# A window of half a microsecond in a rehearsed order of five engines

## The chip, the cores and the metric

The kernel runs on one core of a Trainium2 chip. The metric is the device time of one execution in microseconds, taken as the median of several runs.

## The reference

A residual stream x of shape (8, 512, 256), so 8 batches of 512 tokens, goes through six blocks. Names in brackets are those of the kernel.

```
x = x + 0.5 * ffn0(layernorm(x))    # f0, round 1: 704 hidden, FP4 quantise/dequantise, silu(gate) * up
x = x + attn0(layernorm(x))         # a0: sigmoid q and k, decaying causal mixing over blocks of 128
x = x + 0.5 * ffn0(layernorm(x))    # f0, round 2
x = x + 0.5 * ffn1(layernorm(x))               # f1, round 1: soft mixture of 8 x 128 slots
x = x + attn1(layernorm(x))                    # a1: 16 heads of 16, causal softmax, LoRA on q, k, v, o
x = x + 0.5 * ffn1(layernorm(x))               # f1, round 2
```

(Each block gets the normalised x.) The parts that matter below:

```
# ffn1
logits = einsum(xn, slots)                       # 512 x 1024 for each batch
slots_in = einsum(xn, softmax(logits, over tokens))
h = gelu(slots_in @ w1);  processed = h @ w2     # hidden 1024
out = einsum(processed, softmax(logits, over slots))
# attn1
scores = q @ k.T / 4 + causal mask;  attn = softmax(scores);  out = lora(attn @ v, wo)
```

## The kernel before

Every stage of every block is written as a generator of **pieces**: a piece is what stands between two `yield`s, some waits followed by some instructions. An engine's program is a list of such generators (parts), for instance `a1_front`, `a1_first`, `a1_maxima`, `a1_second`, `a1_values` and `a1_out` on TensorE (PE), with counterparts on ScalarE (ACT), VectorE (DVE), GpSimd (POOL) and on SyncE (SP), which issues all DMAs. Within a part the order is fixed. Between the parts of one engine nothing is fixed: when the kernel is built, `rehearse` decides it.

`rehearse` plays the five programs against one another in a model (class `Rehearsal`: a duration for each operation; `LAG`: how long after an instruction its semaphore is seen, 200 ns for PE and 2200 ns for a DMA, whose issue costs 60 ns of SP). In `rehearsal`, each step looks at all pieces whose signals are known to come, on all engines; `start` tells when a piece could begin (its engine free, its semaphores come, its PSUM bank given back, 1283 ns more where ACT's table must change). The piece with the smallest pair (start, due time) is placed next. In the first of ten rounds the due time is the one written at the `yield`; in each later round it is what `latest` found, the latest finish that would not have moved the end of the round before. The order of the round with the shortest modelled end is kept, and `perform` writes each engine's instructions out in it. On the chip each engine runs its instructions in that order and stops at each wait that isn't yet met, with all that stands behind it. No time of the model remains, only the order.

The round 1 blocks f0 and a0 run first, batch by batch; then f0 round 2 mixed with f1 round 1; then a1 mixed with f1 of both rounds, and last f1 round 2 alone.

Two chains of a1 are used below. The matmul helper `three` (lines 714 to 716) makes each product from three f16 matmuls; transposes are on line 720.

- **The Q move.** `a1_front` projects q and k of a batch in two halves of the heads (c = 0, 1): `psum<-a1xT,a1wqh`. ACT and DVE write them to the staging tile a1st, and SP (`a1_moves`, line 689) spreads them into a1Q and a1K with six DMAs each. The move for half c of a batch may start only when the second-pass scores of the batch before have read that half (semaphore a1_s2), and the projection of the other half waits for the move (semaphores a1_q0, a1_q1), since it reuses the staging tile.
- **The maxima's move.** `a1_first` (line 990, with the masks on line 970) computes scores for DVE's row maxima; DVE puts them in a1mt, PE transposes them (`a1_maxima`), ACT copies them to a1mr (line 1404), and SP writes them with four DMAs (line 697) into a row of a1Q (semaphores a1_m0, a1_m1). `a1_second` (line 1020) computes the scores again, now less their maximum, for ACT's exponential (a1PT, line 1415). Its first group of a half waits for that move. Line 1043 is probabilities times values, lines 1139 to 1141 are f1's sums over tokens, and line 1122 spreads f1's column maxima.

Of the kernel before, what the change touches and what calls it, by code (L numbers as in the profile page):

```python
# [263 lines left out]


LAG = {"pe": 200.0, "act": 130.0, "dve": 110.0, "pool": 100.0, "sp": 2200.0}
ROUNDS = 10


# [19 lines left out]
def rehearse(programs, sems):  # L289

    late, best = None, None
    for _ in range(ROUNDS):
        order, end, late = rehearsal(programs, sems, late)
        if late is None:
            break
        if best is None or end < best[1]:
            best = order, end
    return best


def latest(done, end):

    users, last = {}, {}
    for i, (key, work, needs) in enumerate(done):
        if key[:2] in last:
            users.setdefault(last[key[:2]], []).append((i, 0.0))
        last[key[:2]] = i
        for j, offset in needs:
            if j != i:
                users.setdefault(j, []).append((i, offset))  # L310
    sources, left, room = {}, [len(users.get(i, ())) for i in range(len(done))], [0.0] * len(done)
    for j, those in users.items():
        for i, offset in those:
            sources.setdefault(i, []).append((j, offset))
    clock = {key[0]: 0.0 for key, _, _ in done}
    ready = {en: [] for en in clock}
    for i, n in enumerate(left):
        if not n:
            ready[done[i][0][0]].append(i)
    out = {}  # L320
    while len(out) < len(done):
        t, _, en, i = min((max(clock[en], room[i]), -i, en, i) for en in ready for i in ready[en])
        ready[en].remove(i)
        clock[en] = t + done[i][1]
        out[done[i][0]] = end - clock[en]
        for j, offset in sources.get(i, ()):
            room[j] = max(room[j], clock[en] - offset)
            left[j] -= 1
            if not left[j]:
                ready[done[j][0][0]].append(j)  # L330
    return out


def rehearsal(programs, sems, late):

    names = {id(v): k for k, v in sems.items()}
    parts, order, clock, table = {}, {}, {}, None
    for en, program in programs.items():
        notes = []
        q = Queue(None, sems, notes)  # L340
        parts[en] = [Part(i, g, notes) for i, g in enumerate(program(Rehearsal(en, names, notes), q, Banks(q)))]
        order[en], clock[en] = [], 0.0
    came, maker, done = {k: [] for k in sems}, {k: [] for k in sems}, []
    port = {"dve": 0.0, "pool": 0.0}

    def due(en, part):
        return part.due if late is None else late.get((en, part.at, part.n), part.due)

    active = {}
    held, freed = set(), {}  # L350
    blocked, ready = {}, {en: [] for en in programs}

    def missing(part):
        own = {}
        for n in part.piece:
            if n[0] == "wait" and n[1] != "dve" and len(came[n[1]]) + own.get(n[1], 0) < n[2]:
                return n[1]
            if n[0] == "op" and n[3]:
                own[n[3]] = own.get(n[3], 0) + n[4]
        return None  # L360

    def file(en, part):
        if part.due is None:
            return
        name = missing(part)
        if name is None:
            ready[en].append(part)
        else:
            blocked.setdefault(name, []).append((en, part))

    def start(en, part):
        t = clock[en]
        for n in part.piece:
            if n[0] == "wait" and n[1] != "dve":
                if len(came[n[1]]) >= n[2]:
                    t = max(t, came[n[1]][n[2] - 1])
            elif n[0] == "take":
                if n[1] in held:
                    return None
                if n[1] in freed:  # L380
                    name, value = freed[n[1]]
                    if len(came[name]) < value:
                        return None
                    t = max(t, came[name][value - 1])
            elif n[0] == "op":
                if n[2] is not None and n[2] != table:
                    t += 1283
                return t
        return t

    for en in programs:
        for part in parts[en]:
            file(en, part)
    while True:
        best = None
        for en in programs:
            for part in ready[en]:
                t = start(en, part)
                if t is not None and (best is None or (t, due(en, part)) < best[0]):
                    best = ((t, due(en, part)), en, part)  # L400
        if best is None:
            break
        (t, _), en, part = best
        began, needs, me, work = t, [], len(done), 0.0
        signals = []
        for n in part.piece:
            if n[0] == "wait":
                if n[1] == "dve":
                    t += 30
                else:  # L410
                    t = max(t, came[n[1]][n[2] - 1])
                    needs.append((maker[n[1]][n[2] - 1], work - 130.0))
            elif n[0] == "take":
                held.add(n[1])
                if n[1] in freed:
                    name, value = freed[n[1]]
                    needs.append((maker[name][value - 1], -200.0))
            elif n[0] == "after":
                held.discard(n[1])
                freed[n[1]] = (n[2], n[3])  # L420
            else:
                if n[2] is not None:
                    table = n[2]
                slow = en == "pe" and active.get(int(t // 3413.3) - 1, 0) < 3060
                if n[5]:
                    active[int(t // 3413.3)] = active.get(int(t // 3413.3), 0) + n[5]
                if n[6]:
                    t = max(t, port["pool" if en == "dve" else "dve"])
                t += 2 * n[1] if slow else n[1]
                work += n[1]  # L430
                if n[6]:
                    port[en] = t
                if n[3]:
                    came[n[3]] += [t + LAG[en]] * n[4]
                    maker[n[3]] += [me] * n[4]
                    signals.append(n[3])
        done.append(((en, part.at, part.n), work, needs))
        clock[en] = t
        order[en].append(part.at)
        ready[en].remove(part)  # L440
        part.step()
        file(en, part)
        for name in signals:
            again = blocked.pop(name, [])
            for en2, part2 in again:
                file(en2, part2)
    left = sorted((p.due, en, p.gen.__name__, p.piece[:3]) for en in programs for p in parts[en] if p.due is not None)
    assert not left or late is not None, (left[:25], held, [v for v in freed.items()])
    if left:
        return order, 0.0, None  # L450
    end = max(clock.values())
    return order, end, latest(done, end)
# [1708 lines left out]
```

## Time and profile before

| | us |
|---|---|
| median of 3 runs | 2682.31 |
| lowest, highest | 2676.18, 2683.8 |
| the profiled execution, its own time | 2685.53 |
| its span in the profile | 2683.7 |
| PE busy | 2355.7 (88%) |
| DVE busy | 1890.2 (70%) |
| ACT busy | 1594.0 (59%) |
| POOL busy | 880.0 (33%) |
| PE's mean granted clock | 0.959 of full speed |

Shares of busy time are means over the whole span. A busy PE counts the time in which a matmul is in the array, so the real spacing of matmuls is read from their starts. The views used below are the page's busy times, a table of stretches of the span, the list of who waited for whom, and the instructions in order of time.

### The profile page before, as it was taken

The numbers are of one execution on the slowest core, as the hardware profiler recorded it, in microseconds if no ns is written. First come the engines' busy times: TensorE is split into PE (matmuls) and PEld (weight loads), VectorE is DVE, ScalarE is ACT, GpSimd is POOL, SyncE is SP. The second block draws the span as 40 slices with busy tenths as digits, with TensorE's granted clock in tenths as the row PEclk, the third lists the DMA queues.
The fourth block names the chain that finished last, engine by engine and source line by source line (L and its number), as shares of the span: only waits on it lengthen the run. The fifth ranks groups of instructions, "written<-read, shape, count | busy, mean of one in ns | idle before, by whom it ended". The sixth has DMA issues, their size and how long they took to land.

```text
span 2683.7 us, 54388 instructions
## 1 busy us (share of the span) xinstructions
PE 2355.7 (88%) x22748; PEld 1802.2 (67%) x22748; DVE 1890.2 (70%) x3345; ACT 1594.0 (59%) x2643; POOL 880.0 (33%) x631
## 2 busy tenths in 40 slices
PE   1788898987999988989898999899897989998997
PEld 1456666666777776667676777576666677776786
DVE  6689999998797967777676767778676665444331
ACT  2244654657667474775656486666576466666653
POOL 0112212212323321362535364544436155122222
PEclk9789999999999999999998999999998999998999
DMA  4000000000000000000000000000000000000000
GB/s 162 26 1 1 1 1 1 1 1 1 1 1 1 1 1 25 4 23 2 13 14 13 14 14 14 13 14 2 33 2 25 10 4 7 9 9 1 9 9 9
DMA packets 34836, 33.07 MB, mean 12 GB/s; under 512 B 7648, under 2 KB 33952, under 8 KB 34592
## 3 DMA queue, kind: packets, MB, share of 16 engines
q1 hardware_dynamic: 34592, 29.60, 3.4%
q8 instruction: 180, 2.95, 0.5%
q14 instruction: 64, 0.52, 0.1%
HBM read 12.54 MB, written 4.19 MB: 6 GB/s over the span
## 4 chain that ended last, share of the span: by engine, by line
PE 65%; DVE 20%; ACT 7%; issue 4%; POOL 2%; SPq 1%; DMA 1%; POOLq 0%; DVEq 0%; ACTq 0%
PE psum L714 17%; PE psum L715 15%; PE psum L716 15%; PE psum L720 5%; PE psum L1139 2%; PE psum L990 2%; PE psum L1141 2%; PE psum L1140 2%; PE psum L1043 2%; PE psum L1020 1%; POOL a1pr L2102 1%; ACT a1PT L1415 1%; DVE f0hT L1722 1%; DVE f1e L1979 1%; DVE a1pr L1864 1%
## 5 line engine op out<-in xcount | busy, mean ns | idle before, releaser
L2115 POOL TENSOR_TENSOR f1hT<-f1g,f1hT 128x512 f16<-128x512 f32 x256 | 308.2, 1209 | 707.1 <-ACT f1hT L1518 706.8
L2102 POOL TENSOR_TENSOR a1pr<-a1PT,a1pr 128x1024 f16<-128x1024 f32 (+1 forms) x176 | 358.2, 2038 | 309.6 <-DVE a1pr L1864 309.6
L714 PE MATMUL psum<-f1sl,f1w1h 128*128 128x256 f16 x1024 | 287.6, 281 | 32.4 <-ACT f1g L1513 18.9
L714 PE MATMUL psum<-f1w2h,f1hT 128*128 128x256 f16 x1024 | 280.5, 274 | 7.1 <-POOL f1hT L2115 5.5
L715 PE MATMUL psum<-f1sl,f1w1h 128*128 128x256 f16 x1024 | 286.6, 280 | 0.0
L716 PE MATMUL psum<-f1sl,f1w1l 128*128 128x256 f16 x1024 | 286.4, 280 | 0.0
L715 PE MATMUL psum<-f1w2l,f1hT 128*128 128x256 f16 x1024 | 279.6, 273 | 0.0
L716 PE MATMUL psum<-f1w2h,f1hT 128*128 128x256 f16 x1024 | 279.6, 273 | 0.0
L1841 DVE TENSOR_REDUCE a1nm<-psum 128x2 f32<-128x768 f32 (+3 forms) x176 | 198.3, 1126 | 76.4 <-PE psum L970 75.3
L2091 POOL TENSOR_TENSOR f0h<-f0Y,f0sc 128x704 f32<-128x704 f32 x64 | 93.2, 1456 | 415.5 <-DVE f0Y L1710 415.5
L1864 DVE CAST a1pr<-a1PT 128x1024 f16<-128x1024 f32 (+1 forms) x176 | 161.8, 924 | 72.0 <-ACT a1PT L1415 56.3
L1513 ACT ACTIVATE f1g<-psum 128x512 f32<-128x512 f32 x256 | 152.4, 595 | 90.2 <-PE psum L716 80.8
L1415 ACT ACTIVATE a1PT<-psum 128x1024 f32<-128x1024 f32 (+1 forms) x176 | 166.5, 946 | 56.3 <-PE psum L970 34.9
L714 PE MATMUL psum<-wguh,f0xT 128*128 128x352 f16 x512 | 166.0, 324 | 34.9 <-DVE f0xT L1676 21.3
L715 PE MATMUL psum<-wgul,f0xT 128*128 128x352 f16 x512 | 165.4, 323 | 0.0
L716 PE MATMUL psum<-wguh,f0xT 128*128 128x352 f16 x512 | 165.1, 322 | 0.0
L1518 ACT ACTIVATE f1hT<-f1g 128x512 f16<-128x512 f32 x256 | 161.5, 631 | 5.5
L1139 PE MATMUL psum<-f1xnh,f1e 128*128 128x257 f16 x512 | 142.4, 278 | 13.6 <-DVE f1d L1975 9.7
L714 PE MATMUL psum<-f1pr,f1eT 128*128 128x256 f16 x512 | 140.0, 273 | 2.9 <-DVE f1pr L2022 2.6
L714 PEld LDWEIGHTS psum<-f1sl,f1w1h 128*128 128x128 f16 x1024 | 102.9, 100 | 58.3 <-ACT f1g L1513 23.8
L1141 PE MATMUL psum<-f1xnh,f1e 128*128 128x257 f16 x512 | 141.3, 276 | 0.0
L1140 PE MATMUL psum<-f1xnl,f1e 128*128 128x256 f16 x512 | 140.4, 274 | 0.0
(315 smaller groups left out, 6864.1 us busy)
## 6 DMA issues: line engine op xcount, KB each, us to landing
a1Q<-a1st SPq DMA_DIRECT2D x96, 64.0 KB, 2.6
a1K<-a1st SPq DMA_DIRECT2D x96, 64.0 KB, 2.6
x<-in_L_attn_x SPq DMA_DIRECT2D x8, 512.0 KB, 7.7
out<-x SPq DMA_DIRECT2D x8, 512.0 KB, 3.0
wslot<-in_L_ffn_w SPq DMA_DIRECT2D x1, 1024.0 KB, 8.7
wraw<-in_L_ffn_w SPq DMA_DIRECT2D x1, 1024.0 KB, 5.7
wslot<-in_L_ffn_slot_embeds SPq DMA_DIRECT2D x1, 1024.0 KB, 8.0
a1Q<-a1mr SPq DMA_DIRECT2D x64, 4.0 KB, 1.7
```

Of the source, the lines that this page charges most:

```text
L714: e.matmul(out, lh, rh, start=start, stop=False)
L715: e.matmul(out, lh, rl, start=False, stop=False)
L716: return e.matmul(out, ll, rh, start=False, stop=stop)
L1139: e.matmul(v[:, 0:D + 1], e1[:, jp % 2, 0, t, es], xn_h[:, t, 0:D + 1], start=t == 0, stop=False)
L1140: e.matmul(v[:, 0:D], e1[:, jp % 2, 0, t, es], xn_l[:, t, :], start=False, stop=False)
L1141: ins = e.matmul(v[:, 0:D + 1], e1[:, jp % 2, 1, t, es], xn_h[:, t, 0:D + 1], start=False, stop=t == NT - 1)
L1415: e.activation(a1["PT"][:, i % 2, :, 0:w], psum[:, 0:2, 0:w], ACT.Exp).then_inc(s["a1_ex"])
L1518: e.activation(hT1[:, 0, 2 * hp:2 * hp + 2, :], g2, ACT.Copy).then_inc(s["f1_hh"])
L1841: e.tensor_reduce(out, src, AX, ALU.max, negate=True).then_inc(s["a1_m"])
L1864: e.tensor_copy(a1["pr"][:, i % 2, 0, :, 0:w], a1["PT"][:, i % 2, :, 0:w]).then_inc(s["a1_ph"])
L2102: e.tensor_tensor(a1["pr"][:, i % 2, 1, :, 0:w], a1["PT"][:, i % 2, :, 0:w], a1["pr"][:, i % 2, 0, :, 0:w], ALU.subtract).then_inc(s["a1_pl"])
L2115: e.tensor_tensor(hT1[:, 1, 2 * hp:2 * hp + 2, :], gg[:, hp % 2, :, :], hT1[:, 0, 2 * hp:2 * hp + 2, :], ALU.subtract).then_inc(s["f1_hl"])
```

## The change

A new constant and a new rule for the choice of the next piece. For each engine, all pieces that can begin within 500 ns of the earliest one are looked at, and the one with the least due time among them is the engine's candidate, even if it begins later. Between engines the candidate with the smallest (start, due time) goes next, as before.

```diff
 LAG = {"pe": 200.0, "act": 130.0, "dve": 110.0, "pool": 100.0, "sp": 2200.0}
+WINDOW = 500.0
 ROUNDS = 10
...
         best = None
         for en in programs:
-            for part in ready[en]:
-                t = start(en, part)
-                if t is not None and (best is None or (t, due(en, part)) < best[0]):
+            can = [(t, part) for t, part in ((start(en, part), part) for part in ready[en]) if t is not None]
+            if can:
+                first = min(t for t, _ in can) + WINDOW
+                t, part = min(((t, part) for t, part in can if t <= first), key=lambda z: (due(en, z[1]), z[0]))
+                if best is None or (t, due(en, part)) < best[0]:
                     best = ((t, due(en, part)), en, part)
         if best is None:
             break
```

No instruction of the stages is added or taken away, apart from ACT's table loads (152 before, 148 after), which depend on the order. Line numbers below line 264 grow by 3. Nearly every stretch of every engine's order differs; two places are shown.

**PE, the end of batch 5's second pass for head half 0, and batch 6's projection of q for half 1.** Before: the last second-pass group of half 0 (first three rows), and the projection that waits for the Q move.

```order
L1020 MATMUL psum<-a1Q,a1K 128x128 [waits s_a1_ex]
L1020 MATMUL psum<-a1Q,a1K 128x128 x7
L970 MATMUL psum<-cst 128x64 x4
L1043 MATMUL psum<-a1V,a1pr 128x33 [waits s_a1_pl]
L1043 MATMUL psum<-a1V,a1pr 128x33 x15
L1122 MATMUL psum<-f1mr,idb 128x128 [waits s_f1_ss]
L1122 MATMUL psum<-f1mr,idb 128x128 x3
L1020 MATMUL psum<-a1Q,a1K 128x128 [waits s_a1_ex,s_a1_m1]
...
L714 MATMUL psum<-a1xT,a1wqh 128x512 [waits s_a1_cl,s_a1_q0]
```

After, the same group and the same projection:

```order
L1023 MATMUL psum<-a1Q,a1K 128x128 [waits s_a1_ex]
L1023 MATMUL psum<-a1Q,a1K 128x128 x7
L973 MATMUL psum<-cst 128x64 x4
L717 MATMUL psum<-f1sl,f1w1h 128x256 [waits s_f1_pl]
...
L717 MATMUL psum<-f1sl,f1w1h 128x256
L718 MATMUL psum<-f1sl,f1w1h 128x256
L719 MATMUL psum<-f1sl,f1w1l 128x256
L717 MATMUL psum<-a1xT,a1wqh 128x512 [waits s_a1_cl,s_a1_q0]
```

Between the group and the projection stood 44 short matmuls; now 84 matmuls of 256 to 512 columns of f1 stand there beside 56 short ones.

**PE, the last batch: the turn of the maxima of half 0, and the first second-pass group.** Before (the group, which waits for s_a1_m0, stands some 200 rows further on):

```order
L720 MATMUL psum<-cst,a1mt 64x128 [waits s_a1_xu,s_a1_mt]
L720 MATMUL psum<-cst,f1u 128x128 [waits s_f1_Tl,s_f1_ex]
L720 MATMUL psum<-cst,f1u 128x128 x3
L990 MATMUL psum<-a1K,a1Q 128x384 [waits s_a1_m]
L990 MATMUL psum<-a1K,a1Q 128x384
L970 MATMUL psum<-cst 128x64 x4
L714 MATMUL psum<-f1sl,f1w1h 128x256 [waits s_f1_pl]
...
L1020 MATMUL psum<-a1Q,a1K 128x128 [waits s_a1_m,s_a1_m0]
```

After:

```order
L723 MATMUL psum<-cst,a1mt 64x128 [waits s_a1_xu,s_a1_mt]
L1142 MATMUL psum<-f1xnh,f1e 128x257 [waits s_f1_ds,s_f1_el,s_f1_nl]
L1143 MATMUL psum<-f1xnl,f1e 128x256
L1144 MATMUL psum<-f1xnh,f1e 128x257
...
L1023 MATMUL psum<-a1Q,a1K 128x128 [waits s_a1_m,s_a1_m0]
L1023 MATMUL psum<-a1Q,a1K 128x128
L973 MATMUL psum<-cst 128x64 x4
```

Twelve matmuls of about 256 columns now stand between the turn and the group that needs its result, where 20 transposes, 168 long matmuls and 36 matmuls of score groups stood.

## Rows read from the trace of the kernel before

**Rows 1.** The page: busy us, share of the span and instructions of each engine.

```profile
PE 2355.7 (88%) x22748; PEld 1802.2 (67%) x22748; DVE 1890.2 (70%) x3345; ACT 1594.0 (59%) x2643; POOL 880.0 (33%) x631
```

**Rows 2.** Stretches of the span: length, busy us (instructions) of each engine, PE's clock, DMA.

```profile
core 0: us, PE busy (x) PEld busy (x) DVE busy (x) ACT busy (x) POOL busy (x), PEclk, DMA share, GB/s
0.00:134.00 134.00, 56.87 (x252) 37.22 (x252) 85.12 (x153) 36.22 (x57) 12.53 (x16) 0.90 0.30 94
134.00:603.00 469.00, 415.09 (x2929) 291.94 (x2930) 433.54 (x854) 248.56 (x424) 100.14 (x91) 0.96 0.00 1
603.00:1073.00 470.00, 430.52 (x3502) 340.18 (x3500) 378.12 (x660) 298.67 (x478) 132.32 (x107) 0.98 0.01 5
1073.00:2214.00 1141.00, 1033.23 (x12503) 792.90 (x12500) 811.88 (x1372) 732.21 (x1222) 517.74 (x323) 0.96 0.04 13
2214.00:2684.00 470.00, 419.97 (x3576) 339.99 (x3570) 181.52 (x311) 278.31 (x464) 117.31 (x95) 0.94 0.02 8
```

**Rows 3.** PE's waits over the span: us in total, times, longest us.

```profile
PE psum L1020 <- ACT a1PT L1415: 32.8, 39, 4.7
PE psum L714 <- DMA a1Q<-a1st: 23.5, 7, 4.6
...
PE psum L990 <- DMA a1K<-a1st: 2.3, 1, 2.3
```

**Rows 4.** PE in order of time: start us, length us, instruction.

```profile
1877.12 0.27 PE L1140 MATMUL psum<-f1xnl,f1e 128*128 128x256 f16 x1
1877.23 0.27 PE L1141 MATMUL psum<-f1xnh,f1e 128*128 128x257 f16 x1
```

**Rows 5.** PE in order of time, idle us before a row in brackets.

```profile
1880.53 0.22 PE L970 MATMUL psum<-cst 64*128 64x64 bf16 x4
...
1887.18 0.61 PE L714 MATMUL psum<-a1xT,a1wqh 128*128 128x512 f16 x1 [4.57 <-DMA a1Q<-a1st]
```

**Rows 6.** SP's queue in order of time, the same place.

```profile
1880.84 4.28 SPq L689 DMA_DIRECT2D a1Q<-a1st  x6
```

**Rows 7.** The page's DMA issues: count, KB each, median us to landing.

```profile
a1Q<-a1st SPq DMA_DIRECT2D x96, 64.0 KB, 2.6
...
a1Q<-a1mr SPq DMA_DIRECT2D x64, 4.0 KB, 1.7
```

**Rows 8.** Stretches behind three of the Q waits, columns as in rows 2.

```profile
1887.00:1890.00 3.00, 2.81 (x8) 1.08 (x9) 0.00 (x0) 0.04 (x1) 1.57 (x1) 0.50 0.32 109
1286.00:1293.00 7.00, 6.28 (x51) 4.32 (x52) 2.37 (x4) 3.44 (x5) 0.25 (x1) 0.52 0.16 54
1463.00:1474.00 11.00, 9.34 (x139) 6.87 (x137) 7.65 (x17) 7.31 (x12) 6.05 (x4) 0.53 0.06 20
```

**Rows 9.** In order of time: the turn of the maxima, the copy, the four issues.

```profile
2114.94 0.30 PE L720 MATMUL psum<-cst,a1mt 128*64 128x128 f32 x1
...
2115.74 0.26 ACT L1404 ACTIVATE a1mr<-psum 64x128 f16<-64x128 f32 x1
2116.03 2.44 SPq L697 DMA_DIRECT2D a1Q<-a1mr  x4
```

**Rows 10.** Groups of instructions: count, busy us, mean ns of one, idle before.

```profile
L1513 ACT ACTIVATE f1g<-psum 128x512 f32<-128x512 f32 x256 | 152.4, 595 | 90.2 <-PE psum L716 80.8 <-POOL f1hT L2115 6.0
L1518 ACT ACTIVATE f1hT<-f1g 128x512 f16<-128x512 f32 x256 | 161.5, 631 | 5.5
L2115 POOL TENSOR_TENSOR f1hT<-f1g,f1hT 128x512 f16<-128x512 f32 x256 | 308.2, 1209 | 707.1 <-ACT f1hT L1518 706.8
L1415 ACT ACTIVATE a1PT<-psum 128x1024 f32<-128x1024 f32 (+1 forms) x176 | 166.5, 946 | 56.3 <-PE psum L970 34.9 <-POOL a1pr L2102 20.5
L1500 ACT ACTIVATE f1eT<-psum 128x512 f16<-128x512 f32 x128 | 76.3, 596 | 64.6 <-PE psum L720 64.1
L2004 DVE TENSOR_TENSOR f1eT<-psum,f1eT 128x512 f16<-128x512 f32 x128 | 87.5, 684 | 48.8 <-ACT f1eT L1500 48.7
```

**Rows 11.** ACT in order of time, around one table load.

```profile
1209.20 0.27 ACT L1431 ACTIVATE a1cT<-psum 128x128 f16<-128x128 f32 x1
1209.49 1.28 ACT L1465 ACT_TABLE_LOAD   x1
1210.78 1.06 ACT L1465 ACTIVATE f1d<-f1d 128x1024 f32<-128x1024 f32 x1
```

## The prediction

> **What bounds the kernel now.** I read the page's busy shares first, then a table of stages, then the waits of PE. The page gives PE 88% of the span, DVE 70%, ACT 59% [rows 1], but these are averages over four stages [rows 2]. Up to 134 us the weights arrive and are prepared: PE is busy 56.9 of 134 us. From 134 to 603 us the f0 and a0 blocks run: DVE is busy 433.5 of 469 us (92%) and sets the pace; PE's gaps there are cover for DVE. From 603 us on PE is the bound (430.5 of 470, 1033.2 of 1141, 420.0 of 470 us), with DVE at 80, 71 and 39%. Total work is the same in the changed kernel, so only idle time and PE's clock can move. PE's idle time from 603 us on is 39.5 + 107.8 + 50.0 = 197.3 us, and its granted clock there is 0.98, 0.96 and 0.94.
>
> The waits of PE in that stretch [rows 3] fall into two sorts. Many small ones wait for ACT, DVE or POOL: 32.8 us in 39 waits for the exponential, to name the largest. A few large ones wait for a DMA: 23.5 us in 7 waits for the move of Q rows, and 2.3 us once for K.
>
> Matmuls of 256 columns start 0.11 us apart [rows 4]. So the order itself tells how much PE work lies between two of its rows: I call that cover. A wait shows where the cover is shorter than the latency that it has to hide. I take latencies from the trace, cover from the order of before and after, and compare the two.
>
> **Part 1: the Q move, a gain.** SP may move the new Q rows only after the last second-pass score group of the earlier head half. In batch 6 (the eight are counted from 0) that group's masks end at 1880.75 [rows 5], SP issues six DMAs from 1880.84 on, which takes 4.28 us [rows 6], the landing adds 2.6 us [rows 7], and PE starts the projection that waits for it at 1887.18: 6.4 us, of which 4.57 were idle. The rehearsal prices such a move at 6 x 0.06 + 2.2 = 2.6 us, so it believes 1 to 3 us of cover to be enough. Before has covers of 4.0, 3.5, 2.2, 5.5, 1.8, 1.1 and 2.2 us at batches 1 to 7. After has 7.1, 16.6, 4.4, 22.0, 7.0, 11.7 and 16.1: the most urgent work (the second pass) is ahead of the projections, which stand later. Against 6.4 us one batch is short, by 2.0. At batch 0 the order changes too: K's cover is 3.9 us, against one activation, one DVE row, six issues and a landing, so some 4 us of stall, where the K wait of [rows 3] now stands with one of the seven Q waits ahead of it. DMA stalls fall from 23.5 + 2.3 = 25.8 to 2.0 + 4 = 6 us: **-20 us**.
>
> After such a stall PE's granted clock is at the lower of its two levels, 1.2 GHz: 0.50 over 1887 to 1890, 0.52 over 1286 to 1293, 0.53 over 1463 to 1474 [rows 8]. That is 1.5 + 3.4 + 5.2 = 10.1 us of full-rate time lost behind three of the seven. The longer spans hold other stalls as well, and new stalls (part 2) bring some back; I take **-8 us**.
>
> **Part 2: the maxima's move, a loss.** The first second-pass group of a batch waits for the turned row maxima: PE transpose, ACT copy, four DMAs of 4 KB. At the last batch the transpose starts at 2114.94 and takes 0.30, the copy ends at 2116.00 and the four issues take 2.44 us from 2116.03 [rows 9]; the last begins 0.6 us before that is over and lands 1.7 us later [rows 7], at 2119.6. That is 4.4 us after the transpose. Before hides this everywhere: its covers are 7.9, 16.4, 18.5, 17.8, 9.0, 21.0, 21.6 and 27.2 us. After, the second pass is the urgent work, and the rehearsal prices the move at 2.4 us and the whole path near 3: the covers are 4.8, 4.5, 2.1, 4.3, 2.5, 7.1, 3.4 and 1.3 us. Shortfalls against 4.4: 2.3 + 0.1 + 1.9 + 1.0 + 3.1 = 8.4 us. Behind the waiting matmul stands all of PE's queue, since an engine runs its rows in order. ACT's copy may also stand behind another piece of 0.6 us or a table load of 1.28 us [rows 11] at one batch or another, which I put at 3 us in all: **+11 us**.
>
> **Part 3: tighter loops, both signs.** An urgent piece is now waited for up to half a microsecond, so PE gets to the consumer with less work done in between. GELU, copy and subtraction take 0.60 + 0.63 + 1.21 = 2.4 us [rows 10]; covers too short for that (under 2.5) rise from 6 to 16 of 256. The exponential takes 0.95 [rows 10]; covers below 0.99 rise from 33 to 46 of 176. The f1 transposes of the second softmax need 0.60 + 0.68 = 1.3 [rows 10]; short ones rise from 16 to 28 of 128. A loop's latency in the trace runs from PE's signal to the signal that PE waits for. Adding the shortfalls of all loops behind the last a0 block in PE's order, at the shortest tenth of each loop's latencies, gives 56 us before and 77 after: **+21 us**. Only 56 of the 171 us of PE's idle time that is not DMA is explained this way; the rest is queueing, a result that waits on ACT or DVE behind less urgent work. The same window shortens that: ACT work between GELU and its copy falls from 0.82 to 0.71 us in the mean, PE work from the first to the second matmul group of the MLP from 8.3 to 7.7, from slots to their transposes from 4.4 to 3.2; between the two DVE steps of the dispatch weights it grows from 5.6 to 6.7. I take a tenth of 171: **-17 us**. The bounds are zero and the 115 us of queueing times a quarter, 29.
>
> **Part 4: the small terms.** In the stage that DVE bounds, the DVE work ahead of the last a0 update grows from 537 to 547 us, and that of f0's second round falls from 936 to 928: a swap of work that must be done anyway, cover for the one being the other. Taken at 0, with 10 us to either side. At the start, 5 us of attention weights leave the stretch of DVE ahead of the last quantised weight; but PE's first gate matmul has 54 us of DVE work ahead of it, where it had 52. Taken at 0, bounds -5 to +5. ACT's table loads fall from 152 to 148: 4 x 1.28 = 5.1 us [rows 11] of an engine that is busy 59%, so **-2 us**.
>
> The Trainium skill ("ScalarE: Activation LUTs", What ACT_TABLE_LOAD costs) adds a drain of 1.38 us to each load, 2.66 in all; here the load starts 0.02 us after the activation ahead of it has ended, and the one behind starts 0.01 us after the load [rows 11], so the rows speak against a drain. By the page the four loads would be 10.6 us of ACT and the term -4 in place of -2.
>
> **Sum.** -20 - 8 + 11 + 21 - 17 - 2 = -15 us. From the profiled execution's 2685.5 us (span 2683.7) that is 2670.5; that execution is 3.2 us above the median of 2682.3, so the forecast is 2667 us, 0.6% faster.
>
> **Rivals.**
> (a) No change: the saved DMA stalls come back. PE reaches the projection later, but what follows it (scores, softmax) was waited for elsewhere, and parts 2 and 3 eat the rest. For it: the work is the same, and the milestones of PE work keep their places within 1% (the end of the last a1 block at 1794 us of PE work before and 1788 after). It gives 2682, +-8.
> (b) Slower: the half microsecond is spent on the engine that is the bound. PE idles by plan for urgent pieces, and queues do not shrink, since what shortens one chain lengthens another (the dispatch weights above). Place: the score and softmax groups between 1073 and 2214 us, where PE waits for the exponential. At the median latencies of the trace in place of the shortest tenth, the shortfalls from 603 us on are 159 us before and 230 after: +71 us in place of +21 - 17. Then -20 - 8 + 11 + 71 - 2 = +52: 2734. With half of that increase it is 2699. It decides once covers lost weigh more than about 30 us net of the queues. The Trainium skill ("Perfetto Trace Analysis", Optimization Strategies) bears on this: the goal is to keep the matmul engine at high utilization. Waiting on purpose on PE goes against it; by that rule the time would be that of this rival, and the trace agrees with the rule so far as PE is busy over 90% from 603 us on.
> (c) Much faster: the queue term is larger, since waits also drop PE's clock. Tripled (-51) and with the clock at 0.98 throughout instead of 0.96 and 0.94 (0.02 x 1141 + 0.04 x 470 = 42 us, half of it taken), the sum is -70 and the time 2612.
> (d) The window does not do what it says: the rehearsal keeps the best of ten rounds by its own model, and its best round may owe nothing to urgency. The covers above differ in one direction at all eight batches, so it does act; I fold this into (a).
>
> **How the numbers follow.** Forecast 0.37, (a) 0.20, (b) 0.33, (c) 0.10. The range has to reach (b) in its milder half and nearly all of (c): 2620 to 2722; the forecast's own range, from its bounds, is 2640 to 2680. Faster by over 0.3% (about what a measurement of this kernel can tell from no change): 0.46; within 0.3%: 0.19; slower: 0.35.
>
> **What would show it.** Right: PE's waits for the Q move fall from 23.5 us to under 8; a new wait of PE for the maxima's rows, 6 to 15 us at several batches; PE busy time unchanged within 10 us. Part 3 is wrong if PE's waits for ACT, DVE and POOL together grow or shrink by over 20 us. Wrong as a whole if PE's idle time from 603 us on does not fall although the Q waits do: then (b). If DVE's idle time before 603 us changes by over 10 us, part 4 was mis-sized.

## The result and the profile after

The changed kernel takes 2636.7 us (median of 4 runs, 2634.7 to 2646.8), beside 2683.1 for the kernel before (median of 4 runs on the same chip): a ratio of 0.9837, interval 0.9803 to 0.987, or 44 us less (35 to 53). The forecast was 2667. Its sign held, and the size was a third of what came: -15 against -44. The whole range (2620 to 2722) held; the forecast's own (2640 to 2680) was missed by 3 us, and the result lies halfway between the forecast and rival (c). The profiled execution took 2637.7 us with a span of 2635.9. In what follows a time difference is always the ratio's, times 2681 to 2683.

The page of the changed kernel, which answers to [rows 1]:

```profile
PE 2349.1 (89%) x22748; PEld 1795.1 (68%) x22748; DVE 1912.8 (73%) x3345; ACT 1594.3 (60%) x2639; POOL 868.2 (33%) x631
```

The same 22748 matmuls are busy for 7 us less. The same stretches of time as [rows 2], columns as there; since the program is now shorter, the last stretch ends at 2635.9:

```profile
0.00:134.00 134.00, 62.18 (x311) 44.37 (x312) 88.76 (x164) 39.76 (x65) 15.24 (x18) 0.85 0.29 94
134.00:603.00 469.00, 408.18 (x2879) 287.60 (x2877) 434.73 (x845) 247.49 (x417) 99.75 (x89) 0.97 0.00 1
603.00:1073.00 470.00, 436.17 (x3510) 337.89 (x3511) 383.98 (x663) 298.81 (x476) 126.04 (x107) 0.96 0.01 5
1073.00:2214.00 1141.00, 1045.66 (x12633) 798.29 (x12632) 830.64 (x1376) 736.71 (x1234) 526.38 (x333) 0.97 0.04 13
2214.00:2684.00 470.00, 396.94 (x3421) 326.91 (x3419) 174.68 (x300) 271.58 (x448) 100.81 (x86) 1.00 0.02 7
```

Nothing is won where DVE is the bound: the last a0 update ends at 571.8 us, before at 567.7, and the first f1 block ends at 796.1, before at 797.0. The last a1 block ends 19.8 us earlier (2255.4 for 2275.2), and what follows is another 28 us shorter. So there are two gains: about 20 us in the a1 stage and the rest behind it.

PE's waits over the span, which answer to [rows 3]:

```profile
PE psum L1023 <- ACT a1PT L1418: 17.0, 27, 1.6
...
PE psum L1046 <- DVE a1c L1886: 10.2, 8, 2.4
...
PE psum L1023 <- DMA a1Q<-a1mr: 1.8, 2, 1.3
...
PE psum L717 <- DMA a1Q<-a1st: 0.3, 1, 0.3
```

The Q wait is gone (23.5 to 0.3 us) and that for the exponential is halved (32.8 to 17.0), while the wait for the context rows (a1c) has grown from 2.0 to 10.2. The wait for the turned maxima, which the prediction put at 11 us, is 1.8.

The stretch from the end of the last a1 block to the end of the program holds the last experts' layers alone. It is the best place to read, since it has some 3000 matmuls in either kernel. Before:

```profile
2275.20:2683.70 408.50, 363.31 (x2991) 296.48 (x2989) 148.31 (x249) 236.54 (x388) 86.19 (x75) 0.95 0.02 8
```

and after:

```profile
2255.40:2635.90 380.50, 356.15 (x3000) 291.11 (x2998) 155.00 (x270) 238.77 (x395) 85.01 (x74) 1.00 0.02 8
```

PE's idle time in it (length less busy) falls from 45.2 to 24.4 us, and its granted clock rises from 0.95 to 1.00, so that nearly the same matmuls (3000 and 2991) are busy for 7 us less.

### The profile page after: what moved, and what is told of

The parts are those of the page before. It is cut to its first block, busy times and chain, and to the rows that moved or that the text cites. A ratio compares the mean times of both kernels' runs of the same rounds, so it can differ in the third digit from the quotient of the medians.

```text
span 2635.9 us, 54364 instructions
## 1 busy us (share of the span) xinstructions
PE 2349.1 (89%) x22748; PEld 1795.1 (68%) x22748; DVE 1912.8 (73%) x3345; ACT 1594.3 (60%) x2639; POOL 868.2 (33%) x631
## 4 chain that ended last, share of the span: by engine, by line
PE 62%; DVE 22%; ACT 7%; issue 4%; POOL 3%; SPq 1%; DMA 1%; DVEq 0%; POOLq 0%; ACTq 0%
PE psum L717 16%; PE psum L719 15%; PE psum L718 15%; PE psum L723 5%; PE psum L1142 2%; DVE a1pr L1867 2%; PE psum L1144 2%; PE psum L1143 2%; PE psum L993 2%; PE psum L1046 2%; POOL a1pr L2105 2%; DVE a1nm L1844 1%; DVE f1d L1978 1%; PE psum L1023 1%; ACT a1PT L1418 1%
## 5 line engine op out<-in xcount | busy, mean ns | idle before, releaser
L2105 POOL TENSOR_TENSOR a1pr<-a1PT,a1pr 128x1024 f16<-128x1024 f32 (+1 forms) x176 | 350.3, 1991 | 428.4 <-DVE a1pr L1867 428.3
L1867 DVE CAST a1pr<-a1PT 128x1024 f16<-128x1024 f32 (+1 forms) x176 | 180.5, 1026 | 67.0 <-ACT a1PT L1418 46.5
L1503 ACT ACTIVATE f1eT<-psum 128x512 f16<-128x512 f32 x128 | 76.0, 594 | 120.1 <-PE psum L723 119.3
```

Source lines behind the costliest of these rows:

```text
L1867: e.tensor_copy(a1["pr"][:, i % 2, 0, :, 0:w], a1["PT"][:, i % 2, :, 0:w]).then_inc(s["a1_ph"])
L2105: e.tensor_tensor(a1["pr"][:, i % 2, 1, :, 0:w], a1["PT"][:, i % 2, :, 0:w], a1["pr"][:, i % 2, 0, :, 0:w], ALU.subtract).then_inc(s["a1_pl"])
```

## The experiments

Line numbers in the runs' rows are up to nine higher than in the kernel before. Where only a window or a price is changed, the rest of the scheduler is that of the changed kernel, and a window of 0 gives the order of before.

### The two gains, one at a time

The first pair uses the window in a last pass of the rehearsal, on one side only of the end of the last a1 block. The window behind it alone:

```diff
-WINDOW = 500.0
+WINDOW, LATER = 0.0, 500.0
+        used = late
...
-            best = order, end
-    return best
+            best = order, end, used
+    order, end, _ = rehearsal(programs, sems, best[2], True)
+    return order, end
...
-                first = min(t for t, _ in can) + WINDOW
+                first = min(t for t, _ in can) + (LATER if final and len(came["a1_xu"]) >= 4 * B else WINDOW)
```

> The order is that of the kernel before on every engine until the last a1 block is rehearsed (PE's first differing instruction is number 20325 of 23374); only behind it does the half-microsecond window act, so only the last experts' layers are in another order. Theory A (about half of the gain is made in the last stage, by the window itself): PE's gaps behind 2214 us fall from 45.5 to about 21 us and its clock loss from 27.5 to about 2, and the time is 2683 - 24 = about 2659. Rival B (the last stage gained only because the state handed over to it by the a1 stage was better, or by luck of the rounds): within 6 us of before, about 2680.

Measured: 0.9933 (0.9912 to 0.9954), -18 us, short of the 24 expected and far from nothing. The same stretch of this run, with the same 2991 matmuls as before:

```profile
2266.80:2655.50 388.70, 351.86 (x2991) 289.66 (x2988) 147.68 (x249) 244.83 (x395) 85.63 (x75) 0.99 0.02 8
```

408.5 us have become 388.7: 8.4 us of it is idle time (45.2 to 36.8), and 11.4 is PE's busy time at a clock of 0.99 in place of 0.95. Not all of the clock is the window's: this execution reached the stretch 8.4 us earlier than before did (2266.8 for 2275.2), in an order that is still the same up to there (see the last section). Which waits went is seen in PE's waits of that stretch, before:

```profile
PE psum L720 <- ACT f1u L1495: 11.7, 9, 2.0
PE psum L714 <- DVE f1pr L2022: 8.5, 8, 1.9
PE psum L1139 <- DVE f1d L1975: 5.5, 6, 2.2
PE psum L714 <- ACT f1g L1513: 4.1, 2, 2.6
```

and with the window behind the last a1 block:

```profile
PE psum L719 <- DVE f1pr L2027: 6.2, 8, 1.4
PE psum L725 <- ACT f1u L1500: 5.3, 4, 1.5
PE psum L725 <- DVE f1d L1951: 4.8, 2, 2.6
...
PE psum L1144 <- DVE f1d L1980: 1.7, 2, 0.9
```

What fell most is the wait for the exponentials that PE turns (f1u, 11.7 to 5.3 us), then those for f1g (4.1 to 1.1, below these rows) and f1pr (8.5 to 6.2); those for f1d, at three lines now, rose from 5.5 to 7.8. They are waits for results of ACT and DVE, where the window lets an urgent piece pass others.

The complement is the same edit with the two numbers exchanged (`WINDOW, LATER = 500.0, 0.0`):

> The complement: the order of the changed kernel until the last a1 block, and no window behind it (PE's first instruction that differs from the changed kernel is number 20544). Theory A (two separate gains that add): the a1 stage's 20 us stay and the last stage's are lost, 2683 - 22 = about 2661. Rival B (the last stage's gain comes with what is handed over to it): close to the changed kernel, 2637 to 2645. If both this and the tail alone stay near 2680, the gains need each other.

Measured: 0.9921 (0.9905 to 0.9937), -21 us. The two halves sum to -39, the whole change is -44 (35 to 53): they add, within what can be measured. By its times rival B falls on both sides: 2664 where it gave about 2680, 2662 where it gave 2637 to 2645. In the profile a part of it stays open. The last stretch of this run, where no window acts, is 398.5 us long, 10 less than before:

```profile
2257.10:2655.60 398.50, 358.55 (x3000) 293.69 (x2997) 155.88 (x270) 230.47 (x390) 85.43 (x74) 0.98 0.02 8
```

Of the 10 us 5 are idle time (45.2 to 40.0) and 5 are busy time at the higher clock. So of the 28 us by which the changed kernel is shorter here, the timed runs give the window in this stretch about 18.

### The Q stalls by themselves

The clean test of part 1 keeps every engine's order as it was before, and takes away only what the wait is for. The wait protects a buffer: the projection of the second head half goes into the `a1st` slot that the first half's move still reads. With a slot for each half it is not needed. The rehearsal still sees the old wait, so it writes the old order.

```diff
+        st2 = sb("a1st2", [P, 2, 2, T], f16)
...
-                    q.wait_ge(f"a1_{'qk'[k_]}{1 - c}", 96 * (b + c))
+                    if isinstance(e, Rehearsal):
+                        q.wait_ge(f"a1_{'qk'[k_]}{1 - c}", 96 * (b + c))
+                    else:
+                        q.wait_ge(f"a1_{'qk'[k_]}{c}", 96 * b)
...
-                    e.activation(a1["st"][:, i % 2, 0, :], psum[:, 2 + i % 2, :], ACT.Copy, scale=(0.25, 1.0)[k] / WS).then_inc(s["a1_sh"])
+                    e.activation((a1["st"], st2)[c][:, k, 0, :], psum[:, 2 + i % 2, :], ACT.Copy, scale=(0.25, 1.0)[k] / WS).then_inc(s["a1_sh"])
```

(and the same two edits where ACT waits, DVE subtracts and SP moves).

> The kernel before, every engine's order kept word for word, but with a second buffer for the projected Q and K rows, so that PE's projections no longer wait for the move of the rows before: the Q stall (23.5 us in 7 waits) is taken away and nothing else. Theory S (my prediction's: such a stall is worth its time and the slow clock behind it): 2681 - 20 to -28, so 2653 to 2661. Rival T (in the a1 stage a stall that goes lets PE run into the next wait, since ACT and DVE are nearly as far behind): PE's waits for the exponential, for POOL and DVE, or for the moved rows at the first pass, grow by 12 to 20 us, and the time is 2672 to 2681.

Measured: 0.9909 (0.9895 to 0.9924), -24 us (20 to 28). By its time theory S holds. PE's waits from 1073 to 2214 us in this run:

```profile
PE psum L1027 <- ACT a1PT L1424: 35.2, 42, 4.7
PE psum L997 <- DVE a1nm L1850: 9.8, 14, 2.7
PE psum L718 <- ACT f1g L1522: 7.3, 8, 3.2
PE psum L1050 <- POOL a1pr L2111: 6.7, 9, 1.3
```

In the kernel before the same four are 31.4, 9.4, 7.4 and 5.3 us, beside 20.8 for the Q move. Of 20.8 us only 5.5 came back at these four. The seventh stall, ahead of this stretch at batch 0, came back whole: where 2.7 us for Q and 2.3 for K stood, PE now stands for 5.5 us before its first score group. And the clock behind the stalls returned in part: the stretch from 1286 to 1293 us of [rows 8], at 0.52 there, is at 1.00 here, that from 1463 to 1474 is at 0.85 for 0.53, and 1870 to 1890 is at 1.00.

```profile
1286.00:1293.00 7.00, 5.21 (x56) 4.37 (x57) 5.80 (x12) 4.46 (x9) 5.20 (x4) 1.00 0.14 48
```

The profiled executions tell where the time went. From 603 us to the end of the last a1 block (2275.2 before, 2253.4 here) PE's idle time fell from 151.8 to 138.9 us and its busy time by 9 us, from 1520.4 to 1511.5. So about half of the stall time was won as idle time, and the higher clock added 9 us; theory S has the sum right, while rival T has a share in it. How much of the 9 us is owed to the stalls is open, since the clock differs by as much between executions of one order (see the last section). Another 6 us lie in the last stretch, in the same order, and are the clock's (see the last section).

### Is it luck of the order?

The rehearsal's lag of PE's signals is set to 201 ns in place of 200, without a window (`"pe": 201.0`, `WINDOW = 0.0`):

> No window; the rehearsal's lag of PE's signals is 201 ns in place of 200, which moves nothing on purpose and still gives another order (PE's from instruction 113 on). It shows how far two equally aimed orders lie apart. Its cover between the last score group and the projection that waits for the moved Q rows is as short as in before (0 to 4.9 us at the batches 1 to 7). Theory (the gain is the window's): the Q waits stay at 20 to 30 us and the time is 2683 +- 8. Rival (the 46 us are luck among orders): orders scatter by as much as the gain, so this one may lie anywhere between 2640 and 2720.

Measured: 1.002 (1.0006 to 1.0034), +5 us, with 22.1 us of Q waits in 8 times. Another order aimed in the same way gives nearly the same time. The same jitter with the window (`"pe": 201.0`, `WINDOW = 500.0`):

> The changed kernel (window 500 ns) with PE's lag at 201 ns in place of 200: the window's second order, as the jittered run was the second order without it. Its cover ahead of the Q projections happens to be 1.3 to 3.5 us, as short as in before, so the Q waits come back in full, 20 to 30 us. Theory W (the window's gain is shorter waits for ACT and DVE, in the a1 and the last stage): 2630 to 2655 all the same, with PE's waits for the exponential near 17 us and not 32. Theory S: 2637 + 23 = 2660. Rival L (luck of orders): 2665 to 2700.

Measured: 0.9916 (0.9895 to 0.9936), -22 us. The Q waits are back and the waits for the exponential stay short:

```profile
PE psum L717 <- DMA a1Q<-a1st: 20.8, 7, 4.5
...
PE psum L1023 <- ACT a1PT L1418: 14.2, 26, 1.8
```

The time alone does not split the theories: 2656 was measured, theory S gave 2660 and theory W at most 2655. PE's idle time by stages does. From 603 us to the end of the last a1 block it is 151.8 us before, 147.2 here (1655.9 less 1508.7) and 129.8 in the changed kernel (1652.4 less 1522.6); behind that block it is 45.2, 28.9 and 24.4. So theory W is right only in the last stage. The changed kernel is 21 us faster than this run, and its Q waits are 20.5 us less. So the waits for the exponential, 32.8 us before, 17.0 after and 14.2 here, bought nothing that others (a1c, 8.5 us here) did not take back, and the Q stalls are what the a1 stage had to give. **That the window removes them is not assured**: the first order under the window did it, the second did not. Half of the -44 us is thus owed to which order came out; two orders with the window lie 22 us apart, two without it 5.

### Which engine must choose?

Behind the last a1 block again, but the window acts on PE's choice alone, or on that of the other four alone. The edit adds `and en == "pe"` (or `en != "pe"`) to the condition of the first experiment.

> As the run with the window behind the last a1 block only, but there it acts on PE's own choice alone; ACT, DVE, POOL and SP take the earliest piece as before (the order of before until PE's instruction 20325). The tail alone with the window on all engines gave a ratio of 0.9933, -17.5 us. Theory Q (the gain is a shorter queue in front of ACT and DVE: the urgent one of two results that lie there is served first): PE's choice adds little, 0 to -5 us, 2677 to 2682. Rival P (PE's choice carries it: it hands the urgent chain's matmuls out first): -12 to -17 us, 2665 to 2670.

> The complement: behind the last a1 block the window acts on ACT, DVE, POOL and SP, and PE takes the earliest piece as before. Theory Q: -12 to -17 us, 2665 to 2670. Rival P: 0 to -5 us, 2677 to 2682. If both reach about -17, either engine's choice is enough, since each rehearsed order then fits itself to the other; if neither does, the two need each other.

Measured: PE alone 0.9976 (0.9965 to 0.9987), -6 us; the others alone 0.9987 (0.9975 to 1.0), -3 us; both together -18. Neither theory holds: each half gives about a third or less. The two seem to need each other, but the 8 us by which they fall short together are only little more than what these intervals can tell (about 7). The stretch behind the last a1 block, PE alone:

```profile
2274.40:2673.00 398.60, 357.16 (x2991) 291.93 (x2988) 147.65 (x249) 249.80 (x399) 85.84 (x75) 0.97 0.02 8
```

and the others alone:

```profile
2274.60:2678.30 403.70, 360.52 (x2992) 294.85 (x2989) 147.73 (x250) 242.40 (x392) 86.62 (x75) 0.96 0.02 8
```

Idle 41.4 and 43.2 us, beside 45.2 without and 36.8 with all. A chain of the softmax passes PE, ACT and DVE in turn, and what it gains at one engine it loses in the next one's queue. That reading fits the rows, but no run shows it link by link.

### The size of the window

`WINDOW = 250.0`:

> Half the window. Cover ahead of the Q projections 4.0, 5.8, 0.9, 2.6, 4.6, 6.4 and 3.9 us (shortfalls 16.7 us). Theory W (a dose: some urgency helps, a microsecond is far too much): between the two, 2645 to 2670. Rival L (orders scatter and the size means little below a microsecond): outside of that.

Measured: 0.9893 (0.9873 to 0.9913), -29 us, with 10.3 us of Q waits. `WINDOW = 1000.0`:

> The window doubled to a whole microsecond. Cover ahead of the Q projections is 20.8 to 28.9 us at all batches, so no Q waits; cover between the turning of the maxima and the first second-pass group is 11.9 us at batch 0 and 0.3 to 3.3 at the other seven, against a path of 4.2 to 4.8. Theory M (cover counted in PE work is a floor; PE's ordinary waits and slow clock lengthen it by 1 to 3 us a batch, as in the changed kernel): the waits for the maxima's rows grow from 2.5 to between 8 and 18 us, and the time is 2645 to 2660. Rival 1 (more urgency is more gain): 2625 to 2637. Rival 2 (PE idles by plan for up to a microsecond, in all loops): 2670 or more, with PE's waits for ACT, DVE and POOL up by over 20 us.

Measured: 1.0261 (1.0243 to 1.0278), **+70 us**. Rival 2 holds. No Q wait is left, and yet it is the slowest of all. PE's waits from 1073 to 2330 us, most of its a1 stage (the last a1 block ends at 2400.5):

```profile
PE psum L1046 <- POOL a1pr L2105: 26.8, 48, 1.0
PE psum L1023 <- ACT a1PT L1418: 25.0, 44, 1.5
PE psum L993 <- DMA a1K<-a1st: 9.9, 3, 3.8
```

and the stretch itself:

```profile
1073.00:2330.00 1257.00, 1113.66 (x12925) 838.38 (x12924) 869.10 (x1433) 778.98 (x1283) 532.14 (x339) 0.93 0.04 12
```

PE waits 48 times for POOL's probabilities, 0.6 us each, where the changed kernel does so 13 times in its a1 stage (8.1 us). I read them as waits by plan, an urgent piece being awaited for up to a microsecond while others could run; none is longer than 1.0 us. The clock is 0.93 where it was 0.97. The loss is not in this stretch alone: before 603 us PE is idle for 148 us (131 before) and has 171 fewer matmuls behind it. The last stage kept its gain: from 2330 us to the end PE is busy for 399.6 of 419.2 us, at a clock of 1.00. Summed over the span, PE's idle time is 355 us (287 in the changed kernel, 328 before), and the time lost to the lower clock, the span times one less its mean granted clock (0.945, 0.966, 0.959), is 151 us (90 and 110). My theory M named a wait of 8 to 18 us for the maxima; in PE and its weight loads it is 3.8 and 5.7 us, wrong.

So the results are 0, -29, -44 and +70 us for windows of 0, 250, 500 and 1000 ns, with one order for each but 0 and 500. The second order at 500 ns gave -22, so these runs do not tell whether 250 or 500 is better; the +70 lies far outside of that scatter.

### The price instead of the window, and both

The rehearsal prices a DMA's issue at 60 ns, and six took 4.28 us [rows 6]. With 600 ns and no window:

```diff
-        return self.note(60)
+        return self.note(600)
```

> No window; one number of the rehearsal's prices is changed instead: the issue of a DMA costs 600 ns, near the measured six issues in 4.28 us, in place of 60. The covers ahead of the Q projections become 6.4, 6.2, 7.0, 4.0, 2.9, 10.3 and 4.2 us, against 6.4 needed, where before has 4.0, 3.5, 2.2, 5.5, 1.8, 1.1 and 2.2. Theory (the Q stalls are worth their time, whoever takes them away): shortfalls fall from 24.6 to 8.3 us, PE's Q waits to about 8 us, the time to 2683 - 16 - 5 = 2662. Rival (saved Q stalls come back elsewhere): Q waits fall just so, and the time stays within 6 us of 2683.

Measured: 0.9922 (0.9901 to 0.9942), -21 us. The Q waits fall to 2.4 us, the time as theory S says. But the place does not: from 1073 to 2214 us PE's idle time is 106.4 us, for 107.8 before, at the same clock of 0.96. Up to 603 us it is 118.5 for 131.0, and from there to 1073 it is 30.5 for 39.5; behind 2214 us the clock is 0.97 for 0.94. The price moves every order, the start's too, so this run does not tell the theories apart; the one with the second buffer does.

> The changed kernel's window with the rehearsal's DMA issue at 600 ns in place of 60. Its order happens to have short covers again ahead of the Q projections: 4.0, 13.5, 2.4, 3.7, 2.6, 3.5 and 4.8 us against 6.4 needed, shortfalls 17.4 us where the changed kernel has 2.0. Theory S (the gain of the a1 stage is the Q stalls'): Q waits come back with 10 to 16 us, the last stage stays fast, and the time is 2637 + 15 = 2652. Rival T (the window's gain in the a1 stage is shorter queues): 2632 to 2642 although the Q waits return.

Measured: 0.9803 (0.9782 to 0.9823), -53 us, 2625.7 us: the fastest kernel of the study. Both theories were too slow. Its Q waits are back in part, short ones:

```profile
PE psum L717 <- DMA a1Q<-a1st: 8.5, 6, 2.8
```

and its last stretch of [rows 2] is as good as the changed kernel's: PE's idle gaps there are 19.7 us (20.7), its clock 1.00. The medians put it 11 us under the changed kernel, and the intervals of the two ratios overlap, so that it is the faster of the two isn't certain. Taking its Q waits away as well, with the second buffer and the same order:

> The order of the run with both the window and the DMA price (2625.7 us), with the second buffer, so without its Q waits of 8.5 us. Theory S: 2626 - 9 = 2615 to 2619. Rival T: 2622 to 2626.

Measured: 0.9812 (0.9792 to 0.9831), -50 us, no gain. The 8.5 us of waits are gone, and nothing is gained: PE's idle time from 1073 to 2214 us is 97.3 us with them and 99.3 without. The time, 2631, is above even rival T's 2622 to 2626. The two ratios can be told apart to within 8 us, so a gain of up to 5 us is not excluded, but theory S's 9 is. Six stalls of 1.4 us in the mean were slack here; seven of 3.4 in the mean (the kernel before) were not.

## Why the prediction was right in sign and too small

**Part 1, Q move (-20, and -8 for the clock): right.** The waits fell by 23.2 us, and the stalls with the clock behind them are worth -24 (20 to 28) in the order of before, for -28 forecast. PE's projections at batches 1 to 7 wait once, 0.3 us. The wait of about 4 us at batch 0 came: PE stands for 3.1 us before its first score group, at 1029.7 (the profile names no releaser for it).

**Part 2, maxima (+11): wrong, by about 9 us.** The path was sized rightly. From the start of PE's transpose to the last landing it takes 4.2 to 4.8 us at the eight batches; the prediction's 4.4 us, which count from the end of the transpose, are 4.7 from its start. What failed is "Shortfalls against 4.4": I compared the path with a cover counted in PE work. A cover is a floor of the time between two rows. To it comes every ordinary wait in between, and every stretch at the lower clock. From the transpose to the first second-pass group 7.3, 9.5, 5.5, 7.7, 4.8, 14.3, 5.2 and 4.4 us went by, of which 0.3 to 3.7 were other waits and up to 2.0 clock. Batch 7 in order of time, where the cover was shortest (1.3 us by the prediction):

```profile
2079.67 0.40 PE L723 MATMUL psum<-cst,a1mt 128*64 128x128 f32 x1 [0.31 <-DVE x L1894]
2080.10 0.27 ACT L1407 ACTIVATE a1mr<-psum 64x128 f16<-64x128 f32 x1
...
2080.39 9.37 SPq L700 DMA_DIRECT2D a1Q<-a1mr  x8
...
2084.03 0.10 PEld L1023 LDWEIGHTS psum<-a1Q,a1K 50*128 50x128 f16 x2 [0.99 <-DMA a1Q<-a1mr]
2084.03 0.23 PE L1023 MATMUL psum<-a1Q,a1K 50*128 50x128 f16 x2 [0.51 <-DMA a1Q<-a1mr]
```

PE's clock in between:

```profile
2081.00:2084.00 3.00, 2.53 (x12) 1.46 (x10) 1.22 (x3) 2.31 (x4) 0.00 (x0) 0.54 0.03 6
```

Twelve matmuls stand 0.21 us apart where [rows 4] have 0.11, so they cover twice the time. PE stood for 0.51 us, where 3.1 were forecast. Its only other wait for these rows is 1.3 us at batch 4, where 1.9 were forecast, and the 3 us booked for a late copy show in no wait for these rows.

**Part 3, tight loops (+21) and queues (-17): wrong, and where most of the missing gain lies.** In the head the two nearly cancel, as forecast: the head alone gives -21, the Q stalls -24. In the last stage they do not, and the window there gives -18. The term was one figure for all stages, "a tenth of 171". Counted in the orders as the prediction counts (an estimate of mine that no view of the profile shows), the shortfalls behind the last a1 block are 17 us before and 16 after, about equal. So what is left there as queueing is 45 - 17 = 28 us before and 24 - 16 = 8 after. By that estimate it fell by 70% in that stage. Elsewhere it hardly moved: from 603 us to the end of the last a1 block PE's idle time less its waits for DMAs is 126.0 us before (151.8 less 25.8) and 124.6 after (129.8 less 5.2, the 3.1 us at batch 0 counted with them). There PE is the bound, with DVE busy 36% and ACT 58% of the stretch (148.31 and 236.54 of 408.5 us). I read this as the reason that an urgent piece can pass others on these engines at no cost; no run varied their load. PE's idle time from 603 us on that is not DMA fell by about 20 us in all (from 171 to 149 or 152, as those 3.1 us are counted), the bound that the prediction set itself for calling part 3 wrong.

I also booked no clock for it. The last stretch went from 0.95 to 1.00; of its 28 us, 21 are idle time and 7 are busy time. I had this only in rival (c). As the run with the window ahead of this stretch only shows, some of it (about 10 us in its profile) is not the doing of the window there.

**Part 4: as forecast.** DVE's idle time before 603 us changed from 84.3 to 79.5 us. ACT's table loads: no wait of PE is put down to one, and ACT's busy time stayed (1594.0 and 1594.3), so no run shows the 2 us.

**The sum by measured terms**: Q stalls with their clock -24, the last stage -18, which leaves -2 of the -44 for all else, less than the intervals can tell from zero. The -24 was measured in the order of before and the -18 behind it; that they may be added is borne out by the two halves (-21 and -18), within the intervals.

**Rival (b)** names a real mechanism, but not at this size of the window, and not quite at its place. At 500 ns PE's waits for the exponential fell and did not grow. At 1000 ns PE loses time by waiting, but for the exponential it still waits less than before (25.0 us for 32.8); what grew is the wait for POOL's probabilities (5.3 to 26.8). That +70 is near the +52 which it had been priced at is chance, since that price was for 500 ns. The rule beside it, from the Trainium skill ("Perfetto Trace Analysis", Optimization Strategies), that the matmul engine's utilization is to be kept high, agrees with these runs: PE is busy 88% of the span before, 89% in the changed kernel and 87% with the microsecond. What failed is my step from it, that to wait on purpose on PE must go against it: at 500 ns PE's busy share rose.

```profile
PE 2394.0 (87%) x22748; PEld 1816.0 (66%) x22748; DVE 1925.6 (70%) x3345; ACT 1646.4 (60%) x2684; POOL 868.2 (32%) x631
```

The share even flatters that kernel: the same 22748 matmuls are busy for 2394.0 us, where they took 2349.1 in the changed one, and the mean granted clock is 0.945, not 0.966.

## What to carry to other kernels

Count a term by stages before it is averaged: here the scheduler's window did nothing for the stage that DVE bounds and little for the small waits of the a1 stage, while PE's idle time nearly halved in the stage where ACT and DVE have room. A cover counted in work is a floor; before a shortfall is booked, add the waits and the slow stretches that already lie in the gap. When an order changes everything at once, keep the order and take away what one wait is for (here a second buffer): it priced the Q stall to within 4 us, where reordered kernels only surrounded the answer. Try the size of such a window: between 500 and 1000 ns the sign turned. And time a second order before a gain is called the rule's: here it kept half of it.

## What the hardware showed beyond expectation

- The same instructions in the same order do not get the same clock. The kernel with the second buffer runs the last stretch in exactly the order of before, and it is granted 0.98 there, not 0.95:

```profile
2253.40:2655.90 402.50, 354.82 (x2991) 291.60 (x2988) 148.31 (x249) 236.05 (x388) 86.29 (x75) 0.98 0.02 8
```

  Its idle time is 47.7 us, and before's 45.2, yet it is 6 us shorter. The same shows ahead of that stretch. Before, the run with the window behind the last a1 block and the two runs with half of it have the same order on PE, ACT, DVE and POOL until that block ends, and it ends at 2275.2, 2266.8, 2274.4 and 2274.6 us. In the second PE is idle as long as in the first (283.2 and 282.8 us) and busy for 9 us less (1983.6 for 1992.4). So between two profiles of one order some 6 to 9 us may be the clock's alone; what makes it differ, no run shows. That is also why the profiles overstate the first experiment: the timed runs give -18 where its two spans differ by 28.
- Stalls are not worth a fixed share of their length. Seven of the Q kind (3.4 us in the mean, 4.6 the longest) gave 24 us (20 to 28) for 23.5, with a slow clock behind them. Six (1.4 in the mean, 2.8 the longest) gave nothing that could be measured (at most 5 us) for 8.5. The two differ in their order too, so length is not shown to be the reason.
